# A recommender tower: layer 0 of the first pairs a tile at a time, form 0 of layer 1 by a load from the third pair on, and ScalarE's work reordered

## The reference

```python
e = jnp.stack([tbl_0[ids[:, 0]], ..., tbl_31[ids[:, 31]]], axis=1)      # 512 x 32 x 16
x0 = xk = e
for W in (W0, W1, W2):                                               # 32 x 32 x 64, then 32 x 64 x 64
    xk = relu(jnp.einsum('bmd,bhd,mhk->bkd', x0, xk, W))
    outs.append(jnp.sum(xk, axis=2))
h = jnp.concatenate([*outs, dense_ctx], axis=1)                       # 512 x 208
h = relu(h @ W_top1 + b_top1); h = relu(h @ W_top2 + b_top2); y = h @ W_top3
```

## Time and profile before

| | |
|---|---|
| median of 3 runs | 351.25 us (350.33 to 354.12) |
| profiled execution | 348.34 us |
| its span | 346.0 us |
| TensorE matmuls (PE) busy | 303.7 us, 88% |
| VectorE (DVE) busy | 268.3 us, 78% |
| GpSimd (POOL) busy | 249.6 us, 72% |
| ScalarE (ACT) busy | 106.0 us, 31% |
| chain that ended last | PE 60%, DMA 18%, DVE 9%, POOL 5% |

### The profile page before, as it was taken

The page is one execution under the profiler, slowest core; times in us unless marked ns, Lnnn a source line. Parts: engine busy times, 40 slices in busy tenths (PEclk is TensorE's granted clock), DMA queues, the critical chain, the costliest instruction groups (busy, mean ns, idle before and its releaser), DMA issues.

```text
span 346.0 us, 4323 instructions
## 1 busy us (share of the span) xinstructions
PE 303.7 (88%) x1482; PEld 112.8 (33%) x1482; DVE 268.3 (78%) x123; ACT 106.0 (31%) x478; POOL 249.6 (72%) x163
## 2 busy tenths in 40 slices
PE   0088578888859999999999999999999999999996
PEld 0044223344213433232333233323233334433435
DVE  0026628999759998999999999999999997981401
ACT  1001201311302342704272427242714277122112
POOL 5777750887978898888889887988891796947000
PEclk9999969999998999999999999999999999999999
DMA  5287577765698389728772976396459232210000
GB/s 181 35 266 161 179 205 226 289 177 110 185 375 200 79 267 361 133 25 309 305 140 49 352 242 132 83 377 204 106 128 355 67 89 66 49 42 2 0 0 0
DMA packets 55165, 56.68 MB, mean 164 GB/s; under 512 B 37894, under 2 KB 43912, under 8 KB 51944
## 3 DMA queue, kind: packets, MB, share of 16 engines
q1 hardware_dynamic: 41272, 39.92, 35.7%
q10 hardware_dynamic: 9776, 15.44, 17.1%
q0 software_dynamic: 4096, 1.06, 2.8%
HBM read 41.33 MB, written 2.10 MB: 125 GB/s over the span
## 4 chain that ended last, share of the span: by engine, by line
PE 60%; DMA 18%; DVE 9%; POOL 5%; issue 4%; SPq 2%; ACT 0%; DVEq 0%; POOLq 0%
PE result L666 53%; DMA r_forms<-x_rows 9%; DMA x_rows<-gathered_rows 7%; DVE z_vector L611 5%; POOL gathered_rows L341 5%; DVE z_vector L618 3%; DMA gathered_rows<-table,row_index 2%; PE left L703 2%; PE result L718 1%; PE y_psum L718 1%; PE result L724 1%; PE y_psum L724 1%; SPq L287 1%; DMA table_base<-base 1%; SPq L272 1%
## 5 line engine op out<-in xcount | busy, mean ns | idle before, releaser
L666 PE MATMUL result<-z_vector,w_sb 128*64 128x512 f32 (+2 forms) x1056 | 212.5, 552 | 18.1 <-DVE z_vector L618 11.9
L611 DVE TENSOR_TENSOR z_vector<-left,r_forms 128x4096 f32<-128x4096 f32 (+3 forms) x44 | 168.3, 3868 | 11.2 <-PE left L703 9.3
L357 POOL TENSOR_TENSOR z_pool<-r_forms,xj_forms 128x2048 f32<-128x2048 f32 (+2 forms) x30 | 127.5, 4273 | 29.6 <-DMA xj_forms<-x_sb 23.6
L341 POOL DMA_INDIRECT gathered_rows<-table,row_index x128 | 121.5, 949 | 37.6 <-issue 35.4
L666 PEld LDWEIGHTS result<-z_vector,w_sb 128*64 128x64 f32 x1056 | 74.4, 139 | 150.6 <-issue 111.6
L618 DVE TENSOR_TENSOR z_vector<-left,r_forms 128x2048 f32<-128x2048 f32 (+4 forms) x52 | 88.8, 1758 | 32.1 <-DMA r_forms<-x_rows 28.3
L666 PE MATMUL result<-z_pool,w_sb 128*64 128x512 f32 (+2 forms) x240 | 51.7, 568 | 2.0 <-POOL z_pool L357 2.0
L420 ACT ACTIVATE x_sb<-result 128x512 f32<-128x512 f32 (+2 forms) x27 | 14.8, 549 | 106.5 <-PE result L666 106.5
L428 ACT ACTIVATE x_sb<-x_sb 128x16 f32<-128x16 f32 x168 | 33.4, 201 | 6.4 <-issue 5.1
L428 ACT ACTIVATION_READ_ACCUMULATOR x_sb<-x_sb 128x1 f32 x168 | 31.5, 188 | 0.0
L584 DVE TENSOR_REDUCE d_sums<-x_sb 128x32 f32<-128x512 f32 (+2 forms) x21 | 12.9, 618 | 23.6 <-ACT x_sb L420 23.6
(11 more groups left out here) (41 smaller groups left out, 44.5 us busy)
## 6 DMA issues: line engine op xcount, KB each, us to landing
r_forms<-x_rows SPq DMA_DIRECT2D x24, 1024.0 KB, 9.9
r_forms<-x_rows SPq DMA_DIRECT2D x8, 768.0 KB, 6.9
xj_forms<-x_sb ACTq DMA_DIRECT2D x24, 256.0 KB, 5.2
h_form<-x_rows SPq DMA_DIRECT2D x12, 256.0 KB, 3.0
xj_form<-x_sb ACTq DMA_DIRECT2D x12, 256.0 KB, 4.3
gathered_rows<-table,row_index POOLq DMA_INDIRECT x128, 3.7
r_forms<-x_rows SPq DMA_DIRECT2D x4, 512.0 KB, 5.4
x_rows<-gathered_rows SPq DMA_DIRECT2D x24, 64.0 KB, 2.9
```

What stands on the lines that cost most here:

```text
L341: nc.gpsimd.indirect_dma_start(gathered_rows[:, half % GATHERED, g], None, table, bass.IndirectOffsetOnAxis(ap=row_index[:, at:at + 1], ax ...
L357: nc.gpsimd.tensor_tensor(z_pool[:, unit % NZP, :, :, 0:columns(p)], r_forms(q, p)[:, :, s0:s1], xj1_forms[form_buffer(n, p)][:, :, 0:colu ...
L611: nc.vector.tensor_tensor(z_vector[:, unit % NV, :, 0:s1 - s0, 0:columns(p)], left[:, bank, :, 0:columns(p)].unsqueeze(2).broadcast_to([12 ...
L666: done = nc.tensor.matmul(result_of(n, p)[K * t:K * t + K, 0:columns(p)], weights, z[:, t, 0:columns(p)], start=first, stop=last)
```

## The change

Six edits, in the words of the code:

1. `layer0_by_tile` takes the place of `vector_unit` and `squares` for layer 0 of pairs 0 and 1. It waits for tile 0's product, issues tile 0's five matmuls, then the same for tile 1.
2. SP interleaves store, h and r0 by tile only for pair 2; pair 1 now has both stores first, then both h, then both r0, as pairs 3 to 8.
3. GpSimd waits for select (1,1) ahead of the last four gathers of pair 2.
4. `BY_LOAD` holds form 0 of layer 1 from pair 2 on, alternating with that of layer 2. All loads share `xj0_form`; the last pair's buffer of its own is gone. TensorE's selects are left for pairs 0 and 1 alone.
5. On ScalarE the load of form 0 for (2,p) goes out after the copy of form 0 for (1,p+1), for p above 0, where it followed the Relu of (1,p).
6. The copies of form 1 for (1,p+1), p above 0, stand ahead of the Relu of (2,p-1) and behind the sums; they followed that Relu and the load behind it. In the last round they stood ahead of the sums.

```diff
-BY_LOAD = [(2, _p) for _p in range(NP - 2)] + [(1, NP - 1), (2, NP - 2), (2, NP - 1)]
+SELECTED = 2
+BY_LOAD = [(2, 0)]
+for _p in range(SELECTED, NP):
+    BY_LOAD += [(1, _p), (2, _p - 1)]
+BY_LOAD.append((2, NP - 1))
...
-                if p <= 2:
+                if p == 2:
...
             for k in range(4):
+                if k == 3:
+
+                    pool.wait_ge(selected, 2)
                 gather(GATHERS_BEFORE[4] + 4 * k, GATHERS_BEFORE[4] + 4 * k + 4)
...
             for p in range(NP - 1):
-                copy_xj1(1, p)
+                if p < 2:
+                    copy_xj1(1, p)
                 if p > 0:
                     copy_xj0(2, p - 1)
                 copy_h(p + 1)
                 relu(1, p)
-                load_xj0(2, p)
+                if p == 0:
+                    load_xj0(2, p)
                 if p == 2:
                     load_top()
                 if p > 0:
                     copy_xj1(2, p - 1)
                 relu(0, p + 1)
-                if p + 1 == NP - 1:
+                if p + 1 >= SELECTED:
                     load_xj0(1, p + 1)
                 load_xj1(1, p + 1)
-                if p + 1 == NP - 1:
+                if p + 1 >= SELECTED:
                     copy_xj0(1, p + 1)
-                    copy_xj1(1, p + 1)
+                    load_xj0(2, p)
                 if p > 1:
                     sum_x3(p - 2)
                 if p > 0:
+                    copy_xj1(1, p + 1)
                     relu(2, p - 1)
                 load_xj1(2, p)
...
+            def layer0_by_tile(p):
+
+                unit = VECTOR_BEFORE[0, p]
+                for t in range(2):
+                    to = result[0][K * t:K * t + K, 0:columns(p)]
+                    pe.wait_ge(z_vector_ready, 2 * unit + 1 + t)
+                    if p > 0 and t == 0:
+                        pe.wait_ge(x_ready[0], p)
+                    for s in range(4):
+                        used = nc.tensor.matmul(to, w0_sb[:, s], z_vector[:, unit % NV, t, s, 0:columns(p)],
+                                                start=s == 0, stop=False)
+                    if t == 1:
+                        used.then_inc(z_vector_used, 1)
+                    pe.wait_ge(z_square_ready, 2 * p + 1 + t)
+                    used = nc.tensor.matmul(to, w0_sb[:, 4], z_square[:, t, 0:columns(p)], start=False, stop=True)
+                used.then_inc(z_square_used, 1)
...
-            vector_unit(0, 0, 0)
-            squares(0)
+            layer0_by_tile(0)
             pe.wait_ge(select_loaded, 16)
             select(1, 0)
             busy(4)
             for p in range(NP - 1):
                 layer(1, p)
-                vector_unit(0, p + 1, 0)
-                squares(p + 1)
+                if p == 0:
+                    layer0_by_tile(1)
+                else:
+                    vector_unit(0, p + 1, 0)
+                    squares(p + 1)
```

More of the change, by code:

```diff
@@ L173, in build @@
         late2 = from_spare(N2 * LATE).rearrange("p (k c) -> p k c", k=N2)
-        xj0_last = z_square
         y_sb = h_form[0:1, 0].rearrange("o (t b) -> o t b", t=2)
@@ L195, in build @@
         xj0_loaded = [sem(f"xj0_loaded_t{t}") for t in range(2)]
-        xj0_last_loaded = [sem(f"xj0_last_loaded_t{t}") for t in range(2)]
         left0_copied = sem("left0_copied")
@@ L412, in relu @@
                     if n < 2:
-                        if n == 0:
+                        if n == 0 and p <= SELECTED:
                             act.wait_ge(selected, p)
                         for t in range(2):
-                            if n == 1:
-                                act.wait_ge(xj0_loaded[t], 16 * p)
+                            if (n + 1, p - 1) in BY_LOAD:
+                                act.wait_ge(xj0_loaded[t], 16 * (BY_LOAD.index((n + 1, p - 1)) + 1))
                             act.wait_ge(xj1_loaded[n][t], 16 * p)
@@ L448, in load_xj0 @@
                 act.wait_ge(x_ready[n - 1], p + 1)
-                if n == 1:
-                    act.wait_ge(z_square_used, NP)
-                elif p > 0:
-                    act.wait_ge(left0_copied, 2 * BY_LOAD.index((2, p - 1)) + 2)
+                load = BY_LOAD.index((n, p))
+                if load > 0:
+                    act.wait_ge(left0_copied, 2 * load)
                 for t in range(2):
                     rows = x_sb[n - 1][K * t:K * t + H, 0:columns(p)]
-                    home, loaded = (xj0_form, xj0_loaded) if n == 2 else (xj0_last, xj0_last_loaded)
-                    act.dma_start(home[:, t, 0:columns(p)], rows.unsqueeze(1).broadcast_to([H, DELTAS, columns(p)])
-                                  ).then_inc(loaded[t], 16)
+                    act.dma_start(xj0_form[:, t, 0:columns(p)],
+                                  rows.unsqueeze(1).broadcast_to([H, DELTAS, columns(p)])
+                                  ).then_inc(xj0_loaded[t], 16)
             def copy_xj0(n, p):
@@ L461, in copy_xj0 @@
                 for t in range(2):
-                    if n == 2:
-                        act.wait_ge(xj0_loaded[t], 16 * (p + 1))
-                    else:
-                        act.wait_ge(xj0_last_loaded[t], 16)
+                    act.wait_ge(xj0_loaded[t], 16 * (BY_LOAD.index((n, p)) + 1))
                     act.wait_ge(z_vector_ready, 2 * VECTOR_BEFORE[before] + 3 + t)
-                    home = xj0_form if n == 2 else xj0_last
-                    nc.scalar.activation(left[:, 0, t, 0:columns(p)], home[:, t, 0:columns(p)], ACT.Copy
+                    nc.scalar.activation(left[:, 0, t, 0:columns(p)], xj0_form[:, t, 0:columns(p)], ACT.Copy
                                          ).then_inc(left0_copied, 1)
```

## The result

The changed kernel took **352.23 us** (median of 20 runs, 350.04 to 354.43); the kernel before, on the same chip, 350.73 (20 runs, 347.73 to 354.12). The ratio is 1.0136 with a 95% interval of [1.0101, 1.0171]. All ratios here leave out executions that fell in a disturbed state, over 1.5% above the fastest of the same kernel. The medians alone give 1.0043, and 1.0136 does not follow from the times listed: their mean after, 352.40, over 1.0136 is 347.67, under the lowest of the 20 before. By none of the three is it faster; on another kind of chip it is, by 0.4 to 0.5% (e5, e13). Forecast were 345.7 and a range of 340.5 to 350.8. The profiled execution after took 353.59 us, span 351.7, against 346.0 before: 5.7 longer.

A forecast was written before the change was run, and what follows sets the result against it. VectorE was taken as the bound until 228 us, with TensorE 0.62 behind, and TensorE in the tail. GpSimd's earlier first product (-4.4) and the tail select (-1.06) gave -5.5 us: 345.7, range 340.5 to 350.8.

The forecast's parts named there:

- Layer 0 of pair 0 by tile: TensorE's layer 0 of pair 0: lone tiles lose overlap, select (1,0) and its gathers 2.0 us later, bounds 0 to 2.4.
- Pair 1 by tile and SP's order: Layer 0 of pair 1: no slow clock, matmuls 6.4 us, gain 2.2, select (1,1) done at 50.4 instead of 52.6.
- X: Start of GpSimd's first product: 55.5 us against 59.95, 4.4 earlier, bounds 51.5 to 57.7.
- The held gathers: GpSimd's last four gathers of pair 2: wait for select (1,1), store at 57.9, VectorE gets r0 0.7 us earlier.
- r0 of pair 3 follows X: GpSimd's queue carries the 4.4 us lead on: r0 of pair 3 lands at 94.4 and 97.2.
- Form 0 by a load at gain 0: Layer 1 from pair 2: six selects of 1.06 us removed, five gain 0, load taken as 3.9 us and covered.
- Rival 4: Slower: form 0 loads of pairs 2 and 3 sit on the path at 9.6 us; +2.9, 354.2 us; chance 10%.
- L: Time of the form 0 loads for pairs 2 and 3: 9.6 us in Rival 4, decisive from 8.1.
- Tail: TensorE's stretch at the end: select (1,7) removed, gain 1.06 us, with 0.3 to spare.
- Steady part: Period per pair of sample blocks stays 33.83 us, VectorE without waits, TensorE idle 1.7 rather than 0.6.
- rival 2: TensorE is the true bound and each of six selects counts: -10.8, 340.4 us; chance 5%.
- ScalarE's moved copies: ScalarE's reordered load and form 1 copies: cost 0; last-round Relu up to 1.2 us later, covered by TensorE's backlog.

The follow-up runs named there:

- e5: The changed kernel unchanged, on a chip where the kernel before takes 355.95 us: 353.63 us, ratio 0.995 to the kernel before.
- e13: The changed kernel unchanged, on a chip where the kernel before takes 355.74 us: 353.67 us, ratio 0.9958 to the kernel before.
- e3: The changed kernel without GpSimd's wait for select (1,1) ahead of the last four gathers of pair 2: 349.25 us, ratio 0.9967 to the kernel before.
- e1: The kernel before with layer 0 of pairs 0 and 1 by tile, SP's new order and the held gathers only: 349.51 us, ratio 0.9943.
- e4: The changed kernel with form 0 of (1,2) from TensorE's select again, loads from pair 3 on: 349.44 us, ratio 0.9971 to the kernel before.
- e10: The changed kernel unchanged, on a chip where the kernel before takes 349.73 us: 353.14 us, ratio 1.0075 to the kernel before.
- e18: The changed kernel, gathers still held, form 0 of pairs 2 to 6 by selects and only pair 7 by a load: 345.76 us, ratio 0.9856.
- e11: The changed kernel without the wait ahead of the last gathers, form 0 of (1,2) by TensorE's select, loads from pair 3 on: 344.76 us, ratio 0.9851.
- e12: The changed kernel without held gathers and with form 0 of layer 1 by a load only from pair 7 on: 343.46 us, ratio 0.9809.
- e15: The changed kernel, gathers still held, form 0 by a load only for pair 7, on a 355.74 us chip: 352.34 us, ratio 0.9915.
- e16: The changed kernel without held gathers, form 0 by a load only for pair 7, on a 355.74 us chip: 353.69 us, ratio 0.9948.
- e14: The changed kernel without GpSimd's wait ahead of the last four gathers, loads kept, on a 355.74 us chip: 354.71 us, ratio 0.9974.
- e8: The changed kernel without held gathers, form 0 of (1,2) by select, form 1 issued first, 12 idle matmuls ahead of pair 2: 359.81 us, ratio 1.008.

## Why the prediction was wrong, step by step

**Layer 0 of pair 0 by tile: right in kind, too dear.** 20 matmuls took 3.67 us (24.85 to 28.52), and the Relu came 0.84 later than before, not 2.0.

**Pair 1 by tile and SP's order: right.** Forecast: no slow clock, select done at 50.4, matmuls 6.4 us. Measured: none there, 48.8, 6.17 us. X was forecast 55.5 and came at 54.5.

**The held gathers, the first step that failed.** I let the four gathers land in 3.7 us and the store behind them find "the queues nearly empty". The last gather, issued at 53.50, was in only at about 60.4. Four form-1 loads and r0 of pair 2, tile 0, had been issued between 47.8 and 49.8; that they slowed it is likely, and no run takes them away. The store went out at 60.40 (forecast 57.9), r0 of tile 1 at 64.45 (61.3), and VectorE had it at 70.70: 2.6 us later than before, where I had 0.7 earlier and a bound of 2. I also priced only the transfer. Its follower was TensorE: 9.16 us idle and then 5.75 us for matmuls of 3.65. The 2.6 and these 2.1 are the 4.7 us by which pair 2's Relu is late. Without the hold (e3) r0 is there at 67.28, with a slow stretch of 6.8 us instead of 10.2. Over the traces of the first kind of chip that have tile-by-tile layers, the Relu starts at 77.3 to 79.7 with the hold (after, e1, e4, e10, e18) and at 75.6 to 75.9 without it (e3, e11, e12).

Even so it is not earlier than the 75.00 of before: the 3.8 us gained at pair 1's Relu (47.32 against 51.16) don't get through layer 0 of pair 2 with or without the hold. In e12 TensorE idles 6.42 us ahead of it and takes 5.13 for its 16 matmuls. The gain can only come by GpSimd.

**"r0 of pair 3 follows X": the second.** I carried GpSimd's lead of 4.4 us straight through its queue, since before it ran with no pause. But its product of pair 2 also needs form 1 of pair 2, and so x of layer 0 of pair 2. Before, that form was in about 5 us early (loads issued after 75.63, 3.9 to land, product at 85.60), which is what a lead of 4.4 uses up. With x 4.7 us later and the loads in front, GpSimd idled 8.89 us and came out 3.4 late instead of 4.4 early; of the 8.89, e1 has 5.60 with the same x and no load in front. That lateness reaches VectorE through r0 of pair 4. In eleven traces of the first kind of chip, all but e12, where VectorE does not wait for it, that row of VectorE starts 45.3 to 48.2 us after GpSimd's first product of pair 2, with the loads and without; here 135.41 less 88.96 is 46.5. I named what the lead would release, but not what else each product waits for.

**Form 0 by a load at gain 0: the third, and the largest.** Its own latency was nearly as forecast: the first copy starts 4.05 us after its load's issue, the first product 5.75 us after it, for 5.1 in the forecast. Two things were left out. Form 1's loads stand behind form 0's on ScalarE's queue: they go out at 81.65, 1.9 us after the Relu, share the transfer with form 0's, and GpSimd is the one that waits. Its product starts 8.0 to 9.3 us after pair 2's Relu with the load in front (after, e3, e10) and 5.3 to 6.0 without (e1, e4, e11, e12, e18). And the next form 0 loads, issued at 86.04, run beside r0 of pair 3, which went out at 88.48, 2.6 us earlier than before where X promised 4.4, and still reached VectorE at 102.31 instead of the forecast 97.2. There it cost only 0.29 us, since VectorE was late itself; the waits for r0 of pairs 4 and later are where time goes. The Trainium skill, DMA: Bandwidth & Descriptors, section Queues, rings and completion order, has each DMA engine take turns between queues with work; the medians of the 1 MB r_forms, 9.1 to 10.1 us without the loads of pairs 3 to 6 and 10.1 to 12.2 with them, agree with it. In size the loads are 1.6 to 2.2% by the table, of which pair 2's is 1.0 to 1.2%. Rival 4 was the nearest in size (354.2), but by another route: by its own sum (first product at the Relu's end plus L plus 1.2) L was 4.6 us, 86.08 less 80.31 and 1.2, under its 8.1, and the load still cost.

**Tail: right**, 1.06. **Steady part: right for one pair**, 33.83 (176.17 to 210.00); rival 2 is dead. TensorE idles 2.4 us in it (31.41 busy), forecast 1.7. The pair before it takes 35.97 us (140.20 to 176.17), with the waits for r0 at 171.33 and 173.96, which I had at nothing. **ScalarE's moved copies:** no run takes them alone. In e12 VectorE waits 2.80 us for ScalarE's copy of form 1 for layer 2 of pair 1 (the row at 108.46). It is not one of the moved copies, and e1, with ScalarE's old order, waits 2.21 for it. Ahead of it ScalarE issues the six loads of the dense network's weights (`load_top`), from 101.65 to 107.32 us in e12: a cost that stood there before and that only a lead of VectorE brings out.

**The sum.** Without the two failed parts (e12) the medians differ by 6.3 us and the profiled spans by 3.9, around the 5.5 I forecast for all of it. That this agrees is in part luck: X leads by 8.3 us there, where I had 4.4, and 3.7 of it are lost at pair 2's form 1, a wait that the working does not have. The front and the tail do gain on this kind of chip; the working's way to the number is not confirmed by it.

## What to carry to other kernels

When a lead is carried along a queue, list for each instruction in it every other input it waits for, and how early that input was; the lead ends at the first that was only just in time. A load in place of 1.06 us of matmuls is not free because its latency is covered: count what stands behind it on its own queue and what shares the DMA engines with it. Work that is held back, "because nothing waits for it now", must be priced at the traffic of its new moment, and an engine left idle by it may pay again in its clock.

## What the runs showed of the hardware

Two of the chips take 355.7 and 356.0 us for the kernel before, where the others take about 350. In all eight kernels traced on them the first Relu starts near 32 us, against 27.2 to 29.0 elsewhere. TensorE's rows there, e15 and then e16 (each fence: TensorE's first and last row of the stage, and ScalarE's Relu):

```profile
24.91 1.95 PE L708 MATMUL result<-z_vector,w_sb 128*64 128x256 f32 x10
...
27.98 0.59 PE L713 MATMUL result<-z_square,w_sb 128*64 128x256 f32 x2
...
31.96 0.38 ACT L424 ACTIVATE x_sb<-result 128x256 f32<-128x256 f32 x1 [9.25 <-remote]
```

```profile
46.88 2.80 PE L705 MATMUL result<-z_vector,w_sb 128*64 128x384 f32 x10
...
51.45 0.81 PE L710 MATMUL result<-z_square,w_sb 128*64 128x384 f32 x2
...
57.68 0.49 ACT L421 ACTIVATE x_sb<-result 128x384 f32<-128x384 f32 x1 [2.63 <-remote]
```

The rows end at 28.57 and 52.26, but the Relus that need them start 3.4 and 5.4 us later, with a releaser that the profile can't name. The ends of matmuls are modelled. Doubling the stages' lengths from their starts gives 24.91 + 2 x 3.66 = 32.23 and 46.88 + 2 x 5.38 = 57.64, where the Relus are. So TensorE ran at half speed there, it seems, at 1.2 GHz, in stretches for which the records grant the full clock. It fits both places, and it is inferred; over all eight traces the same doubling misses the first Relu by 0.0 to 0.8 us, and by 1.4 in e13. It would also say why the corners don't separate on that chip: in e15 the Relu of pair 1 starts at 51.20, in e16 at 57.68, and that alone is larger than what the hold costs. e13 and e14 stand the same way (52.11 and 59.14). Both late ones are without the hold, and so is e8 on the other chip, which is not late (53.68), so whether leaving it out brings this on is open. The kernel before was never traced on such a chip, so whether its late start is the same stays open, as does e8.
